# One-input reductions for the softmax shift, normalisation's short steps on GpSimd, and the attention output gathered with the heads inside

## The chip, the cores and the metric

One core of one Trainium2 chip runs the whole kernel. The metric is the device time of one launch in microseconds (us), lower is better. Work is spread over TensorE (PE), VectorE (DVE), ScalarE (ACT), GpSimd (POOL) and the DMA queue that SyncE (SP) fills; each has its own instruction stream and waits for the others by semaphores.

## The reference

A Macaron block on x of shape (4, 1024, 256) in float32: half a gated feed-forward network, attention, half the same network again.

```python
def ffn(x):                       # weights are ternary, 704 hidden units
    g = (x @ gate_w.T) * gate_s
    u = (x @ up_w.T) * up_s
    return (silu(g) * u) @ down_w.T * down_s
def attn(x):                      # 16 heads of 16, rotary embedding, causal
    q, k, v = heads(x @ Wq.T), heads(x @ Wk.T), heads(x @ Wv.T)
    q, k = rope(q), rope(k)
    att = softmax(q @ k.T / 4 + causal_mask)
    return (att @ v).merge_heads() @ Wo.T
x = x + 0.5 * ffn(layernorm(x))
x = x + attn(layernorm(x))
x = x + 0.5 * ffn(layernorm(x))
```

## The kernel before

**Pieces and their order.** The work is cut into pieces such as `pe_s` (scores), `act_exp` or `dma_oc`. `timetable()` gives each piece a place (a due time), a cost and the pieces it waits for; `Timetable.settle()` then plays the program through with these costs and writes for each of the five engines one fixed order. An engine runs its list strictly in order, so a piece whose input is late holds up everything behind it. Constants steer the result: `MODE_PLACE` (the price for TensorE of changing the array's shape), `WINDOW` (how far it may look ahead), `AHEAD` (how early the scores are due), and `WARM_SHARE`: where TensorE would be busy for less than that share, `warm()` puts in a filler, a product of the identity with itself (L848), whose result nobody reads.

**Stages.** Eight chunks of 512 rows go through the first FFN, with the projections of batch 0 laid into it. Then come 16 attention groups (4 batches, 4 groups of 4 heads), and eight chunks of the second FFN. Projections of the next batch are spread over the attention groups.

**Normalisation, `x_pass`.** Per chunk VectorE takes `bn_stats` (L1108) and `bn_aggr` (L1112) and adds EPS to the variance (L1115, piece `dve_va`); GpSimd raises it to -1/2 (L1246, `pool_rs`); VectorE multiplies mean and result (L1120, `dve_nb`); ScalarE normalises (L1015, `act_xn`) and TensorE transposes (L855). Each x is then split into a high part (ScalarE, XH) and a rest (VectorE, XL, L1125).

**One attention group.** TensorE computes the scores with rows as queries (L932, with mask products L942), only so that VectorE can take each row's maximum (L1200, `dve_max`). The negative maxima are split into a high part and a rest and transposed (`dve_nm`: L1209, L1212, L1214, L1219), written to memory (`dma_nw`, L1398) and read back as two extra rows of Q (`dma_nm`, L1405), against which K has two rows of ones. TensorE computes the scores again, transposed and already shifted (L957); ScalarE takes the exponential into PT (L1080); GpSimd zeroes the diagonal blocks (L1299, `pool_mask`); TensorE multiplies by V (L974), which also yields the row sums. There are eight PSUM banks for all of this.

**The way of the output.** ScalarE copies the result to OS (L1088). SP writes it to DRAM (`ow`, L1411), reads the row sums back (`rs`, L1418), VectorE takes their reciprocal (L1225, `dve_rc`), SP writes that (`rw`, L1424) and then issues `oc`: the outputs of four heads into OC and the reciprocals, repeated 16 times, into SC:

```python
src = OD[c2].rearrange("(h r) q -> h r q", h=4)
sy.dma_start(oc[r, :], src[:, 0:HD, :]).then_inc(sem, 16)
sy.dma_start(sc_[r, :], RD_[c2].unsqueeze(1).broadcast_to([4, HD, 512])).then_inc(sem, 16)
```

GpSimd multiplies the two (L1306, `pool_on`), ScalarE makes the high part (L1093, `act_lh`), GpSimd the rest (L1311), and TensorE projects. There are 16 such `pool_on` in the program. SP's queue also carries Q and K of coming groups (`ld`, L1391, 8 transfers of 192 KB a group) and the rotated projections (`zw`, L1380).

Of the kernel before, what the change touches and what calls it, by code (L numbers as in the profile page):

```python
# [9 lines left out]
F32R = mybir.dt.float32r  # L10
# [73 lines left out]
INNER = {"dve_va": ("dve_bn", "dve_ag"), "dve_nm": ("dve_mn", "dve_nh", "dve_nl"), "pool_r": ("pool_ts", "pool_tc"), "dve_flagint": ("dve_flagsum",)}  # L84
# [14 lines left out]
def s_width(t, ch):  # L99
    return 512 if ch < t // 4 else (t % 4 + 1) * P  # L100
# [31 lines left out]
class Timetable:  # L132
# [21 lines left out]
    def settle(self):  # L154
# [76 lines left out]
        while todo or ends:  # L231
# [12 lines left out]
            for e in self.order:  # L244
                while free[e] <= now:
# [53 lines left out]
MODE_PLACE, WAIT_NS, DMA_RATE, WINDOW = 1.14, 80, 200.0, 56.5  # L299
# [50 lines left out]
def timetable():  # L350
# [22 lines left out]
    def x_pass(who, c, at):  # L373
# [254 lines left out]
def macaron(nc, x_in, wgu, wd, wqkv, wo, gsc, usc, dsc, ident_in, cos_in, sin_in, mask_in, out):  # L628
    ctx = ExitStack()
    with ctx:  # L630
# [37 lines left out]
        NP = [place(f"NP{i}", [P, 2, BT, 4]) for i in range(2)]  # L668
        NM = [place(f"NM{i}", [P, 2, 2, 2, 2, 4], F32R) for i in range(2)]
# [154 lines left out]
        def shift_parts(gr, c2, part):  # L824
            return NM[gr % 2][:, c2, :, part, :, :].rearrange("p a b t -> p t a b")

# [165 lines left out]
        def scalar_program(e):  # L992
            sc = nc.scalar
            for piece in plan.order["ACT"]:
# [12 lines left out]
                elif kind == "act_xn":  # L1007
# [3 lines left out]
                    e.wait_ge("dve_nb", who, c)  # L1011
# [83 lines left out]
        def vector_program(e):  # L1095
            ve = nc.vector
            for piece in plan.order["DVE"]:
                kind, a = piece[0], piece[1:]
                if kind == "dve_va":
# [13 lines left out]
                    ins.then_inc(S["dve_ag"], 1)  # L1113
                    e.wait_ge("dve_ag", *a)
                    ve.tensor_scalar(VE[k], MV[k][:, :, 1], EPS, None, ALU.add).then_inc(S["dve_va"], 1)  # L1115
                elif kind == "dve_nb":
                    who, c = a
                    k = slot["ST", a]
                    e.wait_ge("pool_rs", *a)
                    ve.scalar_tensor_tensor(NB[k], MV[k][:, :, 0], -1.0, RS[k], ALU.mult, ALU.mult).then_inc(S["dve_nb"], 1)  # L1120
# [68 lines left out]
                elif kind == "dve_max":  # L1189
                    gr, t, ch, u, hh = a  # L1190
                    n, sel = s_width(t, ch), 0 if ch == t // 4 else 1
# [3 lines left out]
                    acc = NP[gr % 2][:, sel, t, :]  # L1195
                    if u == "a":
                        acc, src = acc[:, 2 * hh:2 * hh + 2], pair("pe_s", *a)[:, :, 0:n]
                    else:
                        acc, src = acc[:, 2 * hh + u:2 * hh + u + 1], bank("pe_s", *a)[:, 0:n]
                    ve.tensor_reduce(out=acc, in_=src, axis=AX, op=ALU.max, negate=True).then_inc(S["dve_max"], 1)  # L1200
                elif kind == "dve_nm":
                    gr, c2 = a
                    t = slice(4 * c2, 4 * c2 + 4)
                    np_ = NP[gr % 2]
# [3 lines left out]
                    if c2:  # L1208
                        ve.tensor_tensor(np_[:, 0, t, :], np_[:, 0, t, :], np_[:, 1, t, :], ALU.min).then_inc(S["dve_mn"], 1)  # L1209
                        e.wait_ge("dve_mn", *a)  # L1210
                    src = np_[:, 0, t, :].rearrange("p t (a b) -> p t a b", a=2)
                    ve.tensor_copy(shift_parts(gr, c2, 0), src).then_inc(S["dve_nh"], 1)  # L1212
                    e.wait_ge("dve_nh", *a)
                    ve.tensor_tensor(shift_parts(gr, c2, 1), src, f32(shift_parts(gr, c2, 0)), ALU.subtract).then_inc(S["dve_nl"], 1)  # L1214
# [328 lines left out]
```

## Time and profile before

| | |
|---|---|
| median of 3 runs | 898.68 us (896.30 to 898.89) |
| the profiled execution: time | 898.62 us |
| its span in the trace | 896.4 us |
| TensorE busy | 837.8 us, 93% of the span |
| VectorE busy | 642.5 us, 72% |
| ScalarE busy | 552.1 us, 62% |
| GpSimd busy | 376.6 us, 42% |
| DMA | 33.9% of 16 engines' span, 89.8 MB |

Busy time counts instructions that run, also while they are stretched by a wait inside them. Fillers count as TensorE busy. Times below are us from the start of the span, 2.2 us of the execution's time lie outside it.

### The profile page before, as it was taken

To read this page: it belongs to the slowest core of one execution; us is meant where nothing else is said; L and a number is where in the kernel's file an instruction comes from. 1 tells how busy PE (TensorE), PEld (TensorE's weight loads), DVE (VectorE), ACT (ScalarE), POOL (GpSimd) and SP (SyncE) were. 2 spreads that over 40 slices of the span, in tenths; PEclk is the share of its full clock that TensorE was granted. 3 is DMA by queue.
4 is the path that set the end of the run, shared out by engine and by line. 5 is a ranking of instruction groups with operands and counts; after the bars stand their busy time and mean duration, and the time that the engine had idled before them with its cause. 6 is when DMAs were issued, how large, how long until landed. Compare 5 with 4: busy or idle time off the path is not lost.

```text
span 896.4 us, 17613 instructions
## 1 busy us (share of the span) xinstructions
PE 837.8 (93%) x6446; PEld 572.6 (64%) x6446; DVE 642.5 (72%) x1305; ACT 552.1 (62%) x1064; POOL 376.6 (42%) x355
## 2 busy tenths in 40 slices
PE   5899999989998999999999999799999999999996
PEld 5788887775655565665555665345555556888885
DVE  5767678886987878888788778678888802565442
ACT  3755655446555747666767747467667886556642
POOL 1757675453332353351252541321332324555553
PEclk9999999999988979999899999799999999999999
DMA  9701232109345264461453615424641111001101
GB/s 313 288 1 68 74 106 85 25 3 225 115 140 153 58 167 125 150 153 64 101 151 126 180 38 157 110 65 87 206 103 50 45 44 37 24 24 36 36 24 49
DMA packets 64644, 89.80 MB, mean 100 GB/s; under 512 B 18604, under 2 KB 30252, under 8 KB 64300
## 3 DMA queue, kind: packets, MB, share of 16 engines
q1 hardware_dynamic: 64412, 88.57, 33.9%
q8 instruction: 54, 0.88, 0.4%
q14 instruction: 34, 0.28, 0.1%
q10 hardware_dynamic: 144, 0.07, 0.0%
HBM read 45.52 MB, written 40.76 MB: 96 GB/s over the span
## 4 chain that ended last, share of the span: by engine, by line
PE 59%; DVE 18%; ACT 8%; DMA 6%; issue 4%; SPq 2%; POOL 2%; DVEq 1%; POOLq 0%; ACTq 0%
PE psum L869 13%; PE psum L974 9%; DVE NP L1200 8%; PE psum L895 8%; PE psum L932 8%; PE psum L838 8%; PE psum L957 7%; DMA SC<-rd_ 3%; ACT PT L1080 3%; PE psum L848 2%; DVE ST L1108 2%; PE psum L855 2%; ACT XN L1015 2%; DVE HF_f L1151 2%; PE psum L942 2%
## 5 line engine op out<-in xcount | busy, mean ns | idle before, releaser
L1200 DVE TENSOR_REDUCE NP<-psum 128x1 f32<-128x512 f32 (+3 forms) x640 | 362.1, 627 | 70.5 <-PE psum L942 43.9
L1080 ACT ACTIVATE PT<-psum 128x512 f32<-128x512 f32 (+2 forms) x640 | 307.3, 577 | 151.5 <-PE psum L957 150.5
L1299 POOL TENSOR_SCALAR_AFFINE_SELECT PT<-PT 128x512 f32<-128x512 f32 x128 | 80.7, 638 | 235.0 <-ACT PT L1080 235.0
L932 PE MATMUL psum<-K,Q 48*128 48x512 f32 (+2 forms) x768 | 154.6, 419 | 9.6 <-DVE NP L1200 6.1
L957 PE MATMUL psum<-Q,K 50*128 50x512 f32 (+2 forms) x768 | 149.6, 417 | 13.8 <-ACT PT L1080 6.7
L869 PE MATMUL psum<-XH,WG_f 128*128 128x512 f32 x352 | 142.9, 406 | 9.6 <-DVE HF_f L1151 6.4
L974 PE MATMUL psum<-PT,V 128*32 128x512 f32 (+3 forms) x1536 | 150.1, 509 | 1.0 <-POOL PT L1299 0.9
L869 PE MATMUL psum<-XL,WG_f 128*128 128x512 f32 x352 | 138.4, 393 | 0.0
L1256 POOL TENSOR_TENSOR HL_f<-HF_f,HH_f 128x512 fp32r<-128x512 f32 x80 | 102.9, 1295 | 80.6 <-ACT HH_f L1044 80.4
L932 PEld LDWEIGHTS psum<-K,Q 48*128 48x128 f32 x768 | 75.2, 191 | 73.7 <-DVE NP L1200 36.9
L1151 DVE SCALAR_TENSOR_TENSOR HF_f<-psum,US,G_f 128x512 f32<-128x512 f32 x96 | 71.1, 750 | 61.2 <-ACT G_f L1034 35.4
L957 PEld LDWEIGHTS psum<-Q,K 50*128 50x128 f32 x768 | 73.9, 192 | 53.4 <-DVE NP L1200 16.8
L1044 ACT ACTIVATE HH_f<-HF_f 128x512 fp32r<-128x512 f32 x96 | 60.1, 630 | 52.4 <-DVE HF_f L1151 51.3
L895 PE MATMUL psum<-WD_f,HH_f 128*128 128x256 f32 x384 | 88.1, 284 | 3.8 <-DVE HH_f L1158 3.1
L1034 ACT ACTIVATE G_f<-psum,GS 128x512 f32<-128x512 f32 x96 | 65.0, 683 | 37.9 <-PE psum L869 37.2
L974 PEld LDWEIGHTS psum<-PT,V 128*32 128x32 f32 x1536 | 40.8, 111 | 71.7 <-issue 52.0
L848 PE MATMUL psum<-IDT 64*128 64x128 f32 (+1 forms) x428 | 77.4, 300 | 9.3 <-ACT PT L1080 5.7
L869 PEld LDWEIGHTS psum<-XH,WG_f 128*128 128x128 f32 x352 | 66.1, 188 | 29.8 <-DVE HF_f L1151 8.5
L895 PE MATMUL psum<-WD_f,HL_f 128*128 128x256 f32 x320 | 78.0, 280 | 0.0
L848 PEld LDWEIGHTS psum<-IDT 64*128 64x128 f32 (+1 forms) x428 | 65.9, 204 | 17.5 <-ACT PT L1080 9.2
L895 PEld LDWEIGHTS psum<-WD_f,HH_f 128*128 128x128 f32 x384 | 69.9, 189 | 7.6 <-issue 6.3
L869 PEld LDWEIGHTS psum<-XL,WG_f 128*128 128x128 f32 x352 | 66.2, 188 | 12.6
(75 smaller groups left out, 1072.6 us busy)
## 6 DMA issues: line engine op xcount, KB each, us to landing
zd<-ZH SPq DMA_DIRECT2D x32, 512.0 KB, 4.8
Q<-zd SPq DMA_DIRECT2D x64, 192.0 KB, 3.9
K<-zd SPq DMA_DIRECT2D x64, 192.0 KB, 5.0
zd<-ZL SPq DMA_DIRECT2D x16, 512.0 KB, 4.8
od<-OS SPq DMA_DIRECT2D x32, 256.0 KB, 3.5
OC<-od SPq DMA_DIRECT2D x32, 128.0 KB
SC<-rd_ SPq DMA_DIRECT2D x32, 128.0 KB
out<-X SPq DMA_DIRECT2D x16, 256.0 KB, 2.1
```

The lines of the kernel that those rows point to most:

```text
L838: ins = tn.matmul(dst, x, w, start=(m == 0), stop=(m == len(terms) - 1))
L848: tn.matmul(bank(*piece)[:, 0:P], IDT[r, :], IDT[r, :], start=True, stop=True)
L869: ins = tn.matmul(bank(*piece), f32(w) if general else w, f32(x) if general else x, start=(kt + m == 0), stop=(kt + m == 2))
L895: ins = tn.matmul(dst, f32(h) if general else h, f32(w) if general else w, start=(n == 0), stop=(n == len(terms) - 1))
L932: ins = tn.matmul(dst, Q[k][r, p, t * P:(t + 1) * P], K[k][r, p, ch * 512:ch * 512 + w], start=(m == 0), stop=not diag)
L957: ins = tn.matmul(dst, K[k][r, p, j * P:(j + 1) * P], Q[k][r, p, 512 * c2 + base:512 * c2 + 512], start=True, stop=True)
L974: ins = tn.matmul(bank(*piece)[32 * h:32 * h + 32, skip:512], V[b % 2][:, col:col + 32], pt_view(gr, c2, j)[:, h, :], start=(j == 0), stop ...
L1080: sc.activation(dst, src, ACT.Exp, scale=0.25).then_inc(S["act_exp"], 1)
L1151: ve.scalar_tensor_tensor(HF[ph][k][ul, :], bank("pe_u", *a)[ul, :], US[ul, i:i + 1], G[ph][k][ul, :], ALU.mult, ALU.mult).then_inc(S["dve ...
L1200: ve.tensor_reduce(out=acc, in_=src, axis=AX, op=ALU.max, negate=True).then_inc(S["dve_max"], 1)
L1256: gp_.tensor_tensor(HL[ph][s][:, :], HF[ph][slot[f"Gf{ph}", a]][:, :], f32(HH[ph][s][:, :]), ALU.subtract).then_inc(S["pool_hl"], 1)
L1299: gp_.affine_select(out=pt, in_=pt, compare_op=ALU.is_ge, fill=0.0, base=0, pattern=[[0, 4], [1, P]], channel_multiplier=-1).then_inc(S["p ...
```

## The change

Four edits. (1) Of `dve_nm` every step but the transpose becomes a `tensor_reduce` with one input: the minimum of two halves, the high part (which is now a negated copy, so one of K's two rows of ones becomes -1), and the rest as the sum over two neighbours. The maxima are written in the order in which they are transposed. (2) The addition of EPS and the product of mean and factor move from VectorE to GpSimd, into `pool_rs`, which now has four instructions; `dve_nb` is gone. (3) `rs`, `rw` and `oc` address their tensors with another outer index: position first, head second, and Wo's rows are permuted on the host to match. (4) In the planner the cost of some pieces and four constants change, and `SPARE` adds 3000 ns to the planned end of `dma_oc` and 1200 ns to that of `dma_rs`.

```diff
-INNER = {"dve_va": ("dve_bn", "dve_ag"), "dve_nm": ...
+INNER = {"pool_const": ("pool_ones",), "dve_va": ("dve_bn",), "pool_rs": ("pool_va", "pool_pw"), "dve_nm": ...
...
-                        end = dma_free + LAG[e]
+                        end = dma_free + LAG[e] + SPARE.get(piece[0][:6], 0)
...
-MODE_PLACE, WAIT_NS, DMA_RATE, WINDOW = 1.14, 80, 200.0, 56.5
+MODE_PLACE, WAIT_NS, DMA_RATE, WINDOW = 1.112, 80, 200.0, 52.283
+SPARE = {"dma_oc": 3000, "dma_rs": 1200}
-AHEAD = 4.3
-WARM_SPAN, WARM_SHARE, WARM_COLD = 2700.0, 0.59, 10000.0
+AHEAD = 4.439
+WARM_SPAN, WARM_SHARE, WARM_COLD = 2700.0, 0.567, 10000.0
...
-        add(at, 1900, "dve_va", who, c, ...
-        add(at, 1070, "pool_rs", who, c, after=[("dve_va", who, c)])
-        add(at, 110, "dve_nb", who, c, after=[("pool_rs", who, c)])
+        add(at, 1750, "dve_va", who, c, ...
+        add(at, 1400, "pool_rs", who, c, after=[("dve_va", who, c)])
...
                     if c2:
-                        ve.tensor_tensor(np_[:, 0, t, :], np_[:, 0, t, :], np_[:, 1, t, :], ALU.min)
+                        ve.tensor_reduce(out=f32(sh[:, 0, :]), in_=NP[gr % 2][:, :, :].rearrange("p s n -> p n s"), axis=AX, op=ALU.min)
...
-                    ve.tensor_copy(shift_parts(gr, c2, 0), src)
+                    ve.tensor_reduce(out=sh[:, 1, :], in_=f32(sh[:, 0, :]).unsqueeze(2), axis=AX, op=ALU.max, negate=True)
...
-                    ve.tensor_tensor(shift_parts(gr, c2, 1), src, f32(shift_parts(gr, c2, 0)), ALU.subtract)
+                    ve.tensor_reduce(out=f32(sh[:, 2, :]), in_=f32(sh[:, 0:2, :]).rearrange("p s n -> p n s"), axis=AX, op=ALU.add)
...
+                    gp_.tensor_scalar(VE[k], MV[k][:, :, 1], EPS, None, ALU.add).then_inc(S["pool_va"], 1)
+                    e.wait_ge("pool_va", *a)
+                    gp_.tensor_scalar(NB[k], MV[k][:, :, 0], -1.0, None, ALU.mult)
+                    gp_.tensor_tensor(RS[k], VE[k], NH, ALU.pow).then_inc(S["pool_pw"], 1)
+                    e.wait_ge("pool_pw", *a)
+                    gp_.tensor_tensor(NB[k], NB[k], RS[k], ALU.mult).then_inc(S["pool_rs"], 1)
...
-                    src = OD[c2].rearrange("(h r) q -> h r q", h=4)[:, HD, :].rearrange("h (a n) -> h a n", n=16)
+                    src = OD[c2].rearrange("(h r) q -> h r q", h=4)[:, HD, :].rearrange("h (a n) -> a h n", n=16)
...
-                    src = OD[c2].rearrange("(h r) q -> h r q", h=4)
+                    src = OD[c2].rearrange("(h r) q -> r h q", h=4)
...
-                    sy.dma_start(oc[r, :], src[:, 0:HD, :]).then_inc(sem, 16)
-                    sy.dma_start(sc_[r, :], RD_[c2].unsqueeze(1).broadcast_to([4, HD, 512])).then_inc(sem, 16)
+                    sy.dma_start(oc[r, :], src[0:HD, :, :]).then_inc(sem, 16)
+                    sy.dma_start(sc_[r, :], RD_[c2].unsqueeze(0).broadcast_to([HD, 4, 512])).then_inc(sem, 16)
```

All orders are settled anew. TensorE's list (of the branch that is taken) has 191 fillers where it had 214, and 1055 changes from one kind of product to the next where it had 1087.

Three places of the order. First VectorE at the start of the program; ROW holds the normalisation's small results, FL the flags that decide which of two branches TensorE takes. Before:

```order
1 L1108 BN_STATS ST_61<-X 128x6 x4
2 L1112 BN_AGGR MV_63<-ST_61 128x2 x4
3 L1115 TENSOR_SCALAR ROW<-MV_63 128x4
4 L1131 TENSOR_REDUCE FL<-RG 128x1 x4
5 L1120 SCALAR_TENSOR_TENSOR ROW<-MV_63,ROW 128x4
6 L1131 TENSOR_REDUCE FL<-RD 128x1 x2
7 L1135 TENSOR_SCALAR FL<-FL 128x6
8 L1108 BN_STATS ST_62<-X 128x6 x4
9 L1112 BN_AGGR MV_64<-ST_62 128x2 x4
10 L1115 TENSOR_SCALAR ROW<-MV_64 128x4
11 L1138 TENSOR_REDUCE CST<-psum 1x1
12 L1140 CAST FLAG<-CST 1x1
```

And of the change:

```order
1 L1111 BN_STATS ST_61<-X 128x6 x4
2 L1115 BN_AGGR MV_63<-ST_61 128x2 x4
3 L1127 TENSOR_REDUCE FL<-RG 128x1 x4
4 L1127 TENSOR_REDUCE FL<-RD 128x1 x2
5 L1121 TENSOR_TENSOR XL_82<-psum,XH_80 128x512
6 L1131 TENSOR_SCALAR FL<-FL 128x6
7 L1121 TENSOR_TENSOR XL_82<-psum,XH_80 128x512
8 L1134 TENSOR_REDUCE CST<-psum 1x1
9 L1136 CAST FLAG<-CST 1x1
```

The result that ScalarE waits for no longer stands on VectorE behind four flag reductions, and the second chunk's statistics stand behind the flag.

Second SP's queue at the ninth `pool_on` (batch 2, first pair of groups); OC and SC are the output transfers, Q and K the `ld` of a coming group. Before:

```order
145 L1424 DMA rd_<-RC_74 128x16
146 L1437 DMA OC_108<-od 64x1x512
147 L1438 DMA SC_109<-rd_ 64x1x512
148 L1437 DMA OC_102<-od 64x1x512
149 L1438 DMA SC_103<-rd_ 64x1x512
150 L1391 DMA Q_92<-zd 48x2x512 x2
151 L1391 DMA K_93<-zd 48x2x512 x2
152 L1391 DMA Q_92<-zd 48x2x512 x2
153 L1391 DMA K_93<-zd 48x2x512 x2
```

The change has the same eight rows at the same numbers, 146 to 153; only their addressing differs.

Third ScalarE at the same place; OH is `act_lh`, PT the exponentials. Before:

```order
353 L1080 ACTIVATE PT_97<-psum 128x512 x3
354 L1088 ACTIVATE OS_101<-psum 128x512
355 L1080 ACTIVATE PT_97<-psum 128x512
356 L1080 ACTIVATE PT_98<-psum 128x384 x2
357 L1093 ACTIVATE OH_111<-OC_102 128x512
358 L1080 ACTIVATE PT_98<-psum 128x384 x2
359 L1080 ACTIVATE PT_96<-psum 128x512 x2
```

And of the change:

```order
355 L1083 ACTIVATE PT_97<-psum 128x512 x3
356 L1091 ACTIVATE OS_101<-psum 128x512
357 L1083 ACTIVATE PT_97<-psum 128x512
358 L1083 ACTIVATE PT_98<-psum 128x384 x3
359 L1096 ACTIVATE OH_111<-OC_102 128x512
360 L1083 ACTIVATE PT_98<-psum 128x384
361 L1083 ACTIVATE PT_96<-psum 128x512 x2
```

OH moves back by one exponential.

## Rows read from the trace of the kernel before

**Rows 1.** The page: the chain that ended last, shares of the span by engine.

```profile
PE 59%; DVE 18%; ACT 8%; DMA 6%; issue 4%; SPq 2%; POOL 2%; DVEq 1%; POOLq 0%; ACTq 0%
```

**Rows 2.** Windows by stage: length, busy us (instructions) by engine, PEclk, DMA share, GB/s.

```profile
203.30:746.80 543.50, 514.79 (x4510) 298.08 (x4510) 422.59 (x864) 358.82 (x745) 177.99 (x198) 0.95 0.42 116
```

**Rows 3.** Timeline of TensorE: start, us, what [idle before <- releaser].

```profile
429.85 0.69 PE L957 MATMUL psum<-Q,K 50*128 50x384 f32 x2 [2.11 <-ACT OS L1088]
530.38 0.50 PE L957 MATMUL psum<-Q,K 50*128 50x256 f32 x4 [1.49 <-ACT PT L1080]
577.66 0.58 PE L848 MATMUL psum<-IDT 64*128 64x128 f32 x1 [5.73 <-ACT PT L1080]
```

**Rows 4.** Timeline, the stall at 572 us, SP, GpSimd and ScalarE.

```profile
565.16 0.51 SPq L1438 DMA_DIRECT2D SC<-rd_  x1
575.31 1.26 POOL L1306 TENSOR_TENSOR OC<-OC,SC 128x512 f32<-128x512 f32 x1 [8.88 <-DMA SC<-rd_]
576.60 0.63 ACT L1093 ACTIVATE OH<-OC 128x512 fp32r<-128x512 f32 x1 [5.70 <-POOL OC L1306]
```

**Rows 5.** Windows with only OC and SC under way, and with `ld`; columns as Rows 2.

```profile
596.50:600.00 3.50, 2.88 (x33) 1.85 (x30) 2.86 (x7) 1.30 (x4) 0.74 (x2) 1.00 0.27 90
603.00:608.00 5.00, 4.74 (x52) 2.89 (x48) 4.75 (x11) 4.08 (x10) 1.87 (x4) 1.00 1.07 203
```

**Rows 6.** Seven windows at TensorE's lower clock: four of them and the sum of all.

```profile
313.80:323.90 10.10, 10.05 (x57) 6.31 (x58) 6.85 (x15) 2.59 (x6) 6.17 (x6) 0.50 0.77 162
429.90:436.70 6.80, 6.80 (x40) 4.79 (x44) 3.61 (x6) 4.74 (x11) 2.82 (x5) 0.51 0.72 173
532.30:535.70 3.40, 3.40 (x20) 3.18 (x19) 0.42 (x1) 1.26 (x2) 2.82 (x4) 0.52 0.04 14
573.30:583.40 10.10, 5.74 (x30) 2.65 (x30) 2.74 (x5) 2.99 (x7) 4.89 (x6) 0.50 0.32 90
...
sum 47.40, PE 42.94 PEld 26.34 DVE 25.24 ACT 14.56 POOL 20.79; mean PE 6.13 PEld 3.76 DVE 3.61 ACT 2.08 POOL 2.97
```

**Rows 7.** Timeline of TensorE, the same product at either clock.

```profile
256.77 0.63 PE L838 MATMUL psum<-XL,WQH 128*128 128x512 f32 x1
...
303.73 0.40 PE L838 MATMUL psum<-XL,WQH 128*128 128x512 f32 x1
```

**Rows 8.** Timeline of TensorE, idle time that VectorE ended.

```profile
252.44 0.80 PE L932 MATMUL psum<-K,Q 48*128 48x256 f32 x4 [1.99 <-DVE NP L1200]
277.07 0.45 PE L932 MATMUL psum<-K,Q 48*128 48x384 f32 x2 [1.62 <-DVE NP L1200]
693.59 0.50 PE L932 MATMUL psum<-K,Q 48*128 48x512 f32 x2 [1.00 <-DVE XL L1125]
```

**Rows 9.** Lines of VectorE: ns min/median/max, first and last start.

```profile
L1214 DVE TENSOR_TENSOR NM<-NP,NM x32: 187/190/2251, 152.1 to 718.3; 128x16 fp32r<-128x16 f32 x32
L1225 DVE RECIPROCAL RC<-SU x32: 209/243/255, 231.8 to 755.4; 128x16 f32<-128x16 f32 x32
```

**Rows 10.** Timeline at the first stretched step.

```profile
249.16 2.36 POOL L1292 TENSOR_TENSOR ZL<-TR,ZH 128x1024 fp32r<-128x1024 f32 x1 [1.52 <-ACT ZH L1051]
249.32 2.25 DVE L1214 TENSOR_TENSOR NM<-NP,NM 128x16 fp32r<-128x16 f32 x1
```

**Rows 11.** Timeline at the start of the program.

```profile
0.80 0.10 POOL L1238 MEMSET CST<- 128x4 f32 x1 [0.29 <-POOLq L1537]
...
6.77 1.03 POOL L1246 TENSOR_TENSOR ROW<-ROW,CST 128x4 f32<-128x4 f32 x1 [3.94 <-DVE ROW L1115]
...
11.42 2.07 ACT L1015 ACTIVATE XN<-X,ROW 128x256 f32<-128x256 f32 x4 [8.89 <-DVE ROW L1120]
...
22.22 0.47 PE L869 MATMUL psum<-XH,WG_f 128*128 128x512 f32 x1 [1.22 <-ACT G_f L1034]
...
31.46 1.93 DVE L1115 TENSOR_SCALAR ROW<-MV 128x4 f32<-128x4 f32 x1
...
34.10 0.50 PE L869 MATMUL psum<-XH,WG_f 128*128 128x512 f32 x1 [2.20 <-DVE HF_f L1151]
```

More of the change, by code:

```diff
@@ L82 @@
            "dve_xo": "dve_out"}
-INNER = {"dve_va": ("dve_bn", "dve_ag"), "dve_nm": ("dve_mn", "dve_nh", "dve_nl"), "pool_r": ("pool_ts", "pool_tc"), "dve_flagint": ("dve_flagsum",)}
+INNER = {"pool_const": ("pool_ones",), "dve_va": ("dve_bn",), "pool_rs": ("pool_va", "pool_pw"), "dve_nm": ("dve_mn", "dve_nh", "dve_nl"), "pool_r": ("pool_ts", "pool_tc"), "dve_flagint": ("dve_flagsum",)}
 DMAS = {"dma_ld": 4, "dma_zw": 3, "dma_nm": 2, "dma_oc": 2, "dma_on": 2, "dma_sp": 2, "dma_w2": 2}
@@ L377, in x_pass @@
         st, xn, x = p.prior["ST", (who, c)], p.prior["XN", (who, c)], p.prior["XA" if (who, c // 2) == ("a", 0) else "X", (who, c)]
-        add(at, 1900, "dve_va", who, c, after=x_ready(who, c) + ([("act_xn",) + st] if st else []))
-        add(at, 1070, "pool_rs", who, c, after=[("dve_va", who, c)])
-        add(at, 110, "dve_nb", who, c, after=[("pool_rs", who, c)])
-        add(at + 2, 4 * 491, "act_xn", who, c, after=[("dve_nb", who, c)] + ([("pe_xT",) + xn + (1,)] if xn else []))
+        add(at, 1750, "dve_va", who, c, after=x_ready(who, c) + ([("act_xn",) + st] if st else []))
+        add(at, 1400, "pool_rs", who, c, after=[("dve_va", who, c)])
+        add(at + 2, 4 * 491, "act_xn", who, c, after=[("pool_rs", who, c)] + ([("pe_xT",) + xn + (1,)] if xn else []))
         for kt in range(2):
@@ L667, in macaron @@
         VE, RS, NB = ([ROW[:, i, n, :] for i in range(2)] for n in range(3))
-        NP = [place(f"NP{i}", [P, 2, BT, 4]) for i in range(2)]
-        NM = [place(f"NM{i}", [P, 2, 2, 2, 2, 4], F32R) for i in range(2)]
+        NP = [place(f"NP{i}", [P, 2, 16]) for i in range(2)]
+        SH = [place(f"SH{i}", [P, 2, 3, 16], F32R) for i in range(2)]
         NMT = [place(f"NMT{i}", [P, 32]) for i in range(2)]
@@ L822, in pt_view, with maxima_of @@
             return PT[(PT_USES * gr + s) % PTN][:, 4 * off:4 * off + 4 * w].rearrange("p (h n) -> p h n", h=4)
-        def shift_parts(gr, c2, part):
-            return NM[gr % 2][:, c2, :, part, :, :].rearrange("p a b t -> p t a b")
+        def maxima_of(gr, t, ch):
+            if t < 4:
+                return f32(SH[gr % 2][:, 0, 0, :]).rearrange("p (a b t) -> p a b t", a=2, b=2)[:, :, :, t]
+            return NP[gr % 2][:, ch, :].rearrange("p (a b t) -> p a b t", a=2, b=2)[:, :, :, t - 4]
         def tensor_program(e, todo, general):
@@ L1010, in scalar_program @@
                     was = prior["XN", (who, c)]
-                    e.wait_ge("dve_nb", who, c)
+                    e.wait_ge("pool_rs", who, c)
                     if was:
@@ L1112, in vector_program @@
                         ins = ve.bn_aggr(MV[k][:, i, :], ST[k][:, i, :])
[L1113 to L1120, printed above, removed]
+                    ins.then_inc(S["dve_va"], 1)
                 elif kind == "dve_xl":
@@ L1190, in vector_program @@
                     gr, t, ch, u, hh = a
-                    n, sel = s_width(t, ch), 0 if ch == t // 4 else 1
+                    n = s_width(t, ch)
                     e.wait_ge("pe_s", gr, t, ch, u)
@@ L1217, in vector_program @@
                         e.wait_ge(*turn_of("nw", gr - 1, c2))
-                    both = f32(NM[gr % 2][:, c2, :, :, :, :]).rearrange("p a b c t -> p (a b c t)")
-                    ve.transpose(NMT[c2][:, :], both).then_inc(S["dve_nm"], 1)
+                    ve.transpose(NMT[c2][:, :], f32(sh[:, 1:3, :]).rearrange("p s n -> p (s n)")).then_inc(S["dve_nm"], 1)
                 elif kind == "dve_rc":
@@ L1238, in gpsimd_program @@
                     gp_.memset(NH, -0.5)
-                    gp_.memset(f32(ONES[:, :]), 1.0)
+                    gp_.memset(f32(ONES[:, :]), 1.0).then_inc(S["pool_ones"], 1)
+                    e.wait_ge("pool_ones")
+                    gp_.memset(f32(ONES[0:1, :]), -1.0)
                     gp_.memset(ONE, 1.0).then_inc(S["pool_const"], 1)
```

23 lines of the change are left out of this document (10 added, 13 removed).

## The prediction

> **What bounds the kernel now.** I read the chain that ended last first [rows 1]: 59% of it is TensorE, 18% VectorE, 8% ScalarE, and 6% are transfers. TensorE is therefore the engine to watch, and the others matter where it waits for them. The windows by stage come next [rows 2]: in the 543.5 us of the attention groups TensorE counts as busy for 514.8, so 28.7 us are idle, and its mean clock there is 0.95 of full. These two things, idle time and the lower clock, are what an edit on other engines can give back; the products themselves stay the same. Then I looked in TensorE's own timeline for the idle stretches of a microsecond and more and for what stands behind each.
>
> Three of them have one story [rows 3]: 2.11, 1.49 and 5.73 us, 9.3 in all, each ended by ScalarE. The longest can be followed [rows 4]. SP issues the last SC transfer at 565.2. GpSimd stands still for 8.88 us and multiplies at 575.3; ScalarE, whose list has OH in front of further exponentials, has waited 5.70 us for it and runs OH at 576.6; only then do PSUM banks come free, and TensorE goes on at 577.7. So a small transfer of output that nobody needs soon holds the exponentials, because both engines run strictly in order. The other two stand behind ScalarE's copy or exponentials in the same way, before 429.85 and 530.38.
>
> Three others are ended by VectorE [rows 8]: 1.99, 1.62 and 1.00 us, 4.6 in all. Behind the first stands one step of `dve_nm` [rows 10]: L1214 handles 16 numbers per partition and takes 2.25 us, and it ends just as GpSimd's subtraction on 1024 columns (249.16 to 251.52) ends. Its usual time is 190 ns, its longest 2251 [rows 9], while the reciprocal with one input of the same size never takes over 255. So what stretches it is that it has two inputs in SBUF while GpSimd works, and maxima queue behind it.
>
> After such stalls TensorE runs slowly: seven windows, 47.4 us long together, show a granted clock of 0.50 to 0.52 [rows 6], the lower of the two levels (1.2 and not 2.4 GHz). One matmul takes 0.63 us there and 0.40 at the full clock [rows 7], so of busy time at the lower clock I count 1 - 0.40/0.63 = 0.37 as lost. Three windows follow the stalls behind ScalarE (6.80 + 3.40 + 5.74 = 15.9 us busy, 5.9 lost). The fourth, at 313.8 (10.05 us busy), follows a wait that no edit aims at. The rest, 42.94 - 10.05 - 15.94 = 17.0 us, follows the three stalls behind VectorE: 6.3 lost.
>
> **The change part by part.**
>
> *Gather with the heads inside (A).* While only OC and SC are under way, the DMA share is 0.27, which is four engines of 16 busy; with `ld` it is 1.07, all of them [rows 5]. The outer index of these transfers is the head, 4 of them. I take it that each head's 16 rows go to one engine, and that with 16 positions outside the same rows go to 16 engines: a quarter of the time. At 575 us four such transfers stood in the four queues, with `ld` behind them; SP's eight rows are the same after the change, so the load is the same and only its spread differs. In the 3.5 us of that first window at 0.27, four transfers of this kind are mostly done, so the two pairs need some 3.5 to 4 us on four engines and 1 on sixteen, where they now also share four engines with a full `ld`. The wait of 8.88 then shrinks to some 2 to 3 us, and `act_lh`, which ScalarE reaches 5.70 us before its input, no longer waits. `SPARE` adds little there: OH moves back by one exponential only. Elsewhere it plans `pool_on` later by its 3 us, which by itself would cover the two shorter stalls. Worth: 9.3 us of idle time + 5.9 of clock = 15.2. From below nothing (if it does not spread), from above this.
>
> The Trainium skill states such a rule in "DMA: Bandwidth & Descriptors", section "Why a DMA increments its semaphore by 16 and not by 1": the number of engines is the largest one up to 16 that divides the slowest dimension of both sides. By it the old form gets 4 and the new one 16, which would make term A whole; without it term A would be nothing. By the same rule the read of the shift (two parts outside) stays on 2 engines and its write on 4, so these keep their queueing. The 0.27 agrees for the old form; no run yet shows the new one.
>
> *One-input steps (B).* Per `dve_nm` three or four steps stay three or four steps. A one-input step of 16 numbers is not in the trace as a `tensor_reduce`; the nearest are the reciprocal at 243 ns and the two-input step's unhindered 190 [rows 9]. Over about 80 steps the bounds are nothing and 80 x 0.05 = 4 us on VectorE, which is 78% busy in the stage, so off the path by most: I take 0. What goes is the stretching: 4.6 us of idle time + 6.3 of clock = 10.9. From below nothing, if a one-input reduction waits as well.
>
> *Normalisation on GpSimd (C).* GpSimd runs three more short steps per chunk, 24 times. From below such a step costs what a 4-column memset costs, 0.10 us, from above what the power costs, 1.03 [rows 11]; both products are of the cheap kind, so I take 0.1 and with hand-overs 0.4 us a chunk. Behind it on GpSimd wait the pieces of the FFN and masks; it is 33% busy in the attention stage, so this is hidden, and where the cover is gone it would be 24 x 0.4 = 10 us, at the most. VectorE loses two steps and one hand-over. At the start this shows: ScalarE gets its first input at 11.42, after four flag reductions on VectorE; with GpSimd's product right after the power (6.77 + 1.03) it is there at about 8.3. TensorE's first real product does not come 3 us earlier, since the flag needs the last weights; of that I count 1.3. The 1.22 us before 22.22 go, because ScalarE's second normalisation now stands behind the first gate. Of the 2.20 before 34.10, 1.93 were one stretched addition of EPS on VectorE (31.46), which is gone: I count 2. Together 4.5; bounds 1 and 6.
>
> [...]
>
> *Planner (D).* 32 changes of product kind less and 23 fillers less. No row shows a change of kind alone: from below it costs nothing, from above as much as a whole product's 0.40 us [rows 7], together 12.8. Since the products stay, I take it near the lower end, and as 0. The fillers stood in time in which TensorE had nothing else; their loss costs nothing while the clock holds.
>
> *What is late next (E).* TensorE has other idle time in the stage: 28.7 less the 13.9 named is 14.8 us, in waits under 1.5 us for the same engines. A stall that is taken away lets TensorE run into the next of these earlier, and the whole order is drawn anew, so some stalls of the old kind will come at new places. Between nothing and all of A + B = 26.1, I take four tenths back, 10.4. This is the choice on which the size hangs most.
>
> Sum: -15.2 - 10.9 - 4.5 + 10.4 = -20.2 us. Against the profiled execution's own 898.6 (0.1 from the median of the runs) that gives 878.4; I forecast 878.
>
> **The rivals.**
>
> *The gather does not get faster (12%).* The 0.27 could be the pace of reading single rows from DRAM, or `ld` on the same queues could be what delays SC. For it: the wait of 8.88 us fell together with `ld`. Against it: the share is level at 0.27 with no `ld` under way. Then A is nothing: 898.6 - 0.6 x 10.9 - 4.5 = 888.
>
> *A one-input reduction is stretched as well (8%).* The change would not do what it says on VectorE. Against it stands the reciprocal's 255 at most. Then B is nothing: 898.6 - 0.6 x 15.2 - 4.5 = 885.
>
> *Nothing is given back (13%).* The stalls were independent. 898.6 - 30.6 = 868.
>
> *The clock falls more often: slower (8%).* With 23 fillers less a gap of 1 us may be followed by a low stretch where it was not before; now seven are. Place: the attention groups, before products that wait for maxima. At 0.37 us lost per busy microsecond at the lower clock, 54 us more of them, about what there is now once more, eat the whole gain, and 62 make it slower by 0.3%. If the mean clock in the stage fell from 0.95 to 0.85, the lower level would hold for 30% of 543.5 us and not 10%: 109 us more, 40 us lost, 898.6 - 20.2 + 40 = 918. Against it: six of the seven low stretches follow stalls of a microsecond and more that the edits remove.
>
> **How the numbers follow.** My forecast, 878 with its neighbours from 870 to 886, has 54%. The rivals above have 12, 8, 13 and 8%, and 5% are left for a gain that a new order eats to within 0.3%. That 0.3%, 2.7 us, is about what a measurement of this kernel can tell from no change; the runs before lie 2.6 us apart. Faster by more than it: 54 + 12 + 8 + 13 = 87%; same 5%; slower 8%. The range holds the forecast, the two partial cases and most of the case without giving back: 864 to 894.
>
> **What would show it.** DMA share near 1.0 and not 0.27 while only OC and SC run; GpSimd's wait for SC (8.88 at the longest) under 3 us, and no ScalarE wait for `pool_on` over 1 us. The three reductions of the shift at 150 to 250 ns with no instance over 300. First normalisation on ScalarE at 8 to 9 us, the first FFN product 1 us or more earlier, no idle stretch over 1 us at 30 to 36 us. A mean clock in the attention groups of 0.96 or more, that stage at about 527 us. The prediction is wrong if new stalls of 2 us and more stand in that stage, or if the clock is below 0.95 there.

## The result, and the profile after

| | before | after |
|---|---|---|
| median | 898.78 us (896.3 to 901.28, 4 runs) | 860.45 us (858.56 to 865.6, 4 runs) |
| the profiled execution: time | 898.62 us | 865.6 us |
| its span | 896.4 us | 863.6 us |

The ratio is 0.9567, 95% interval 0.9525 to 0.9608: 38 us less, where the prediction said 20 and its range ended at 864. The execution that was profiled is the longest of the four, with a mean clock of 0.987; two others had 0.995 and 0.996 and spans of 857.

The page of the changed kernel, busy time by engine and the chain that ended last [rows 1 before]:

```profile
PE 823.4 (95%) x6400; PEld 561.6 (65%) x6400; DVE 614.7 (71%) x1257; ACT 548.5 (64%) x1064; POOL 391.6 (45%) x428
PE 73%; DVE 13%; ACT 9%; issue 2%; POOL 2%; DMA 1%; SPq 1%; DVEq 0%; POOLq 0%; ACTq 0%
```

TensorE went from 59% to 73% of the chain, and transfers from 6% to 1%. The windows by stage say where it was gained (columns as Rows 2):

```profile
0.00:204.90 204.90, 186.74 (x1106) 156.46 (x1107) 135.95 (x292) 113.92 (x190) 129.55 (x142) 0.98 0.32 107
204.90:712.60 507.70, 494.75 (x4442) 282.64 (x4446) 410.20 (x852) 354.19 (x742) 179.29 (x213) 0.99 0.48 124
712.60:863.60 151.00, 141.88 (x857) 122.52 (x856) 68.60 (x113) 80.42 (x135) 82.78 (x74) 0.98 0.10 32
```

The attention groups take 507.7 us where they took 543.5 [rows 2]: 35.8 less, with 12.95 us idle where there were 28.7, and a clock of 0.99 where it was 0.95. The stages around them, 203.3 and 149.6 us before, are 1.6 and 1.4 us longer. The whole gain lies in the attention groups, and the normalisation's new place shows no gain in the two stages that do it most.

The way of the output, GpSimd, ScalarE and SP (timeline, the same ninth `pool_on` as in [rows 4]; SC's first transfer of the pair there is issued at 564.75):

```profile
564.75 0.59 SPq L1438 DMA_DIRECT2D SC<-rd_  x1
568.99 0.59 SPq L1438 DMA_DIRECT2D SC<-rd_  x1
573.04 1.27 POOL L1306 TENSOR_TENSOR OC<-OC,SC 128x512 f32<-128x512 f32 x1
574.35 0.63 ACT L1096 ACTIVATE OH<-OC 128x512 fp32r<-128x512 f32 x1 [1.49 <-POOL OC L1306]
```

GpSimd no longer waits for SC; its multiplication follows its masks at once. ScalarE still waits 1.49 us, for GpSimd's order and not for a transfer. Over the program, from the list of waits (us in total, times, longest):

```profile
POOL OC L1306 <- DMA SC<-rd_: 6.0, 3, 3.6
ACT OH L1096 <- POOL OC L1306: 5.8, 4, 2.6
```

Before, these were 38.1 us in 13 waits (the longest 11.0, and not the 8.88 that I took for it) and 17.4 us in 8. The longest of each is over the bound that the prediction gave (3.6 for 3 us, 2.6 for 1 us), though both sums fell to a third or less. The DMA share while OC and SC alone run (windows of one microsecond, columns as Rows 2):

```profile
538.50:539.50 1.00, 1.00 (x14) 0.72 (x16) 1.00 (x4) 1.00 (x3) 0.00 (x0) 1.00 0.58 164
566.00:567.00 1.00, 0.99 (x15) 0.63 (x16) 1.00 (x5) 1.00 (x3) 0.00 (x0) 1.00 0.63 150
566.00:566.25 0.25, 0.24 (x5) 0.17 (x2) 0.25 (x2) 0.25 (x2) 0.00 (x0) 1.00 0.97 156
```

Nine to ten of 16 engines are busy in the mean of such a microsecond and not four [rows 5]. The share near 1.0 that I had named holds for a quarter of a microsecond (the last row) and not for longer: SP needs 0.5 to 0.6 us to issue each of the two transfers. That the first is mostly done when the second starts is my reading, and no row separates the two.

The shift's steps (lines of VectorE, ns min/median/max, as Rows 9):

```profile
L1204 DVE TENSOR_REDUCE SH<-NP x16: 177/188/189, 187.1 to 681.7; 128x16 f32<-128x32 f32 x16
L1206 DVE TENSOR_REDUCE SH<-SH x32: 157/170/171, 149.5 to 681.9; 128x16 fp32r<-128x16 f32 x32
L1208 DVE TENSOR_REDUCE SH<-SH x32: 186/186/191, 149.7 to 682.1; 128x16 f32<-128x32 f32 x32
```

None of 80 lasts over 191 ns, where a two-input step lasted up to 2251 [rows 9]. The largest idle stretch of TensorE in the groups is 0.76 us, after the one of 3.11 with which they begin.

### The profile page after: what moved, and what is told of

It is laid out like the page before. It is cut to its first block, busy times and chain, and to the rows that moved or that the text cites. A ratio compares the mean times of both kernels' runs of the same rounds, so it can differ in the third digit from the quotient of the medians.

```text
span 863.6 us, 17536 instructions
## 1 busy us (share of the span) xinstructions
PE 823.4 (95%) x6400; PEld 561.6 (65%) x6400; DVE 614.7 (71%) x1257; ACT 548.5 (64%) x1064; POOL 391.6 (45%) x428
## 4 chain that ended last, share of the span: by engine, by line
PE 73%; DVE 13%; ACT 9%; issue 2%; POOL 2%; DMA 1%; SPq 1%; DVEq 0%; POOLq 0%; ACTq 0%
PE psum L872 15%; PE psum L977 13%; PE psum L935 10%; PE psum L841 10%; PE psum L898 9%; PE psum L960 9%; DVE NP L1196 4%; ACT PT L1083 3%; DVE SH L1196 3%; PE psum L851 3%; PE psum L945 2%; PE psum L858 2%; ACT XN L1018 2%; DVE ST L1111 1%; ACT G_f L1037 1%
## 5 line engine op out<-in xcount | busy, mean ns | idle before, releaser
L1196 DVE TENSOR_REDUCE NP<-psum 128x1 f32<-128x512 f32 (+2 forms) x448 | 260.3, 643 | 31.1 <-PE psum L945 22.0
L960 PE MATMUL psum<-Q,K 50*128 50x512 f32 (+2 forms) x768 | 147.2, 411 | 10.8 <-ACT PT L1083 7.9
L935 PE MATMUL psum<-K,Q 48*128 48x512 f32 (+2 forms) x768 | 146.8, 408 | 4.2 <-DVE SH L1196 1.3
L977 PE MATMUL psum<-PT,V 128*32 128x512 f32 (+3 forms) x1536 | 145.2, 496 | 0.2 <-ACT PT L1083 0.2
L1196 DVE TENSOR_REDUCE SH<-psum 128x2 f32<-128x256 f32 (+2 forms) x192 | 102.5, 590 | 16.2 <-PE psum L945 15.3
L935 PEld LDWEIGHTS psum<-K,Q 48*128 48x128 f32 x768 | 70.2, 184 | 66.3 <-DVE NP L1196 22.1
L960 PEld LDWEIGHTS psum<-Q,K 50*128 50x128 f32 x768 | 71.1, 187 | 53.9 <-DVE NP L1196 15.1
L851 PE MATMUL psum<-IDT 64*128 64x128 f32 (+1 forms) x382 | 67.9, 296 | 4.2 <-DMA IDT<-ident 3.4
```

The source lines that it names most:

```text
L851: tn.matmul(bank(*piece)[:, 0:P], IDT[r, :], IDT[r, :], start=True, stop=True)
L935: ins = tn.matmul(dst, Q[k][r, p, t * P:(t + 1) * P], K[k][r, p, ch * 512:ch * 512 + w], start=(m == 0), stop=not diag)
L960: ins = tn.matmul(dst, K[k][r, p, j * P:(j + 1) * P], Q[k][r, p, 512 * c2 + base:512 * c2 + 512], start=True, stop=True)
L977: ins = tn.matmul(bank(*piece)[32 * h:32 * h + 32, skip:512], V[b % 2][:, col:col + 32], pt_view(gr, c2, j)[:, h, :], start=(j == 0), stop ...
```

## The experiments

E1 to E4 ran on one chip in one series, likewise E5 to E8, E9 to E12, E13 to E16, and E17 and E18, each beside runs of the kernel before (898.1, 898.1, 899.4, 898.8 and 900.8 us). A ratio is to those runs, with its 95% interval in brackets. "Order of before" means that every piece stands where it stood and only operations or addresses differ.

**E1: the gather alone, order of before.**

```diff
-src = OD[c2].rearrange("(h r) q -> h r q", h=4)
+src = OD[c2].rearrange("(h r) q -> r h q", h=4)
```

(and the same for SC, `rs`, `rw`, and Wo's rows.) 

> The kernel before with the third edit alone (rs, rw and oc addressed with the position outside; Wo's rows permuted), every piece in its old place. Theory 1, the forecast's term A at full size: only the three stalls behind ScalarE go, 898.8 - 15.2 = 884, 4 us to either side. Theory 2, the slow spread also held the other transfers that share its engines (the shift's write and read, the loads): more than the named stalls goes, 875 or less. Theory 3, the gather matters little while the order is the old one, since the new order did the work: 892 or more. In all of them the DMA share with only OC and SC under way goes from 0.27 to about 1.

878.86 us, ratio 0.9823 (0.9765 to 0.9881): 10.7 to 21.1 us less, 16 in the middle and 19 by the medians. Term A's 15.2 stands within that, and so does a gain some us larger. TensorE's timeline shows what stayed:

```profile
253.01 0.50 PE L932 MATMUL psum<-K,Q 48*128 48x256 f32 x4 [1.99 <-DVE NP L1200]
276.27 0.44 PE L932 MATMUL psum<-K,Q 48*128 48x384 f32 x2 [1.60 <-DVE NP L1200]
353.43 0.51 PE L957 MATMUL psum<-Q,K 50*128 50x512 f32 x2 [1.49 <-DVE NP L1200]
```

The two long stalls behind VectorE are there almost to the hundredth (1.99 and 1.62 before, [rows 8]; its third, of 1.00, is 0.53), and the three behind ScalarE [rows 3] are gone. The third row shown here has its like in the trace of before and was not in my list. There it stands behind a stretched step too:

```profile
356.31 1.21 DVE L1214 TENSOR_TENSOR NM<-NP,NM 128x16 fp32r<-128x16 f32 x1
358.39 0.50 PE L957 MATMUL psum<-Q,K 50*128 50x512 f32 x2 [1.50 <-DVE NP L1200]
```

**E2: one-input steps alone, order of before.** The edit is the `dve_nm` part of the diff. 

> The kernel before with the first edit alone (the shift by one-input reductions), every piece in its old place. Theory 1, term B at full size: 898.8 - 10.9 = 888, 4 us to either side. Theory 2 (the gather does most): 893 or more, because steps stretched by GpSimd cost TensorE only the three stalls named, and their successors are late for other reasons. Theory 3, the new order did the work: 893 or more as well. In all of them no step of the shift lasts over 300 ns.

886.79 us, ratio 0.9876 (0.9828 to 0.9924): 6.8 to 15.4 less, 11 in the middle, term B's 10.9. The 80 reductions of the shift last 192 ns at the most. In the timeline the stalls behind VectorE are gone, that of 1.50 us too, and those behind ScalarE are left:

```profile
414.41 0.69 PE L960 MATMUL psum<-Q,K 50*128 50x384 f32 x2 [2.41 <-ACT OS L1091]
515.77 0.50 PE L960 MATMUL psum<-Q,K 50*128 50x256 f32 x4 [1.44 <-ACT PT L1083]
562.01 0.58 PE L851 MATMUL psum<-IDT 64*128 64x128 f32 x1 [4.64 <-ACT PT L1083]
```

This shows that the three reductions aren't stretched. It doesn't show that the number of inputs is what counts, since the edit replaced a copy (L1212) as well, which has one input. The trace of before has that copy held too, and so has the addition of EPS, with one input and a constant (lines of VectorE, as Rows 9, and the timeline of one case):

```profile
L1212 DVE CAST NM<-NP x32: 171/182/1303, 151.3 to 718.1; 128x16 fp32r<-128x16 f32 x32
L1115 DVE TENSOR_SCALAR ROW<-MV x24: 170/170/1930, 6.5 to 812.5; 128x4 f32<-128x4 f32 x24
393.63 1.29 POOL L1286 TENSOR_TENSOR TR<-TR 128x512 f32<-128x512 f32 x1
393.65 1.30 DVE L1212 CAST NM<-NP 128x16 fp32r<-128x16 f32 x1
```

**E3: both, order of before.** 

> The kernel before with the first and the third edit, every piece in its old place. If the two add up, it is before less the sum of the two single gains. With the forecast's give-back of four tenths it would be 883; with nothing given back 872.6 for the forecast's sizes. If it is below 866, the two edits explain nearly the whole result of 860 to 862 and the planner's part is small; if it is above 880, the new order gave more than either.

863.91 us, ratio 0.9641 (0.9590 to 0.9692): 27.7 to 36.8 less, 32 in the middle and 34 by the medians. The single gains add up to 27 by the ratios and 30 by the medians. So nothing is given back: with four tenths back even the upper ends of both single intervals, 36.5, would leave 22. Whether the two together are worth more than apart is within the spread. After the stretch of 2.62 us with which the groups begin there is none of a microsecond in them, and the profiled clock is 0.993.

**E4: SPARE and the constants alone.**

```diff
+                        end = dma_free + LAG[e] + SPARE.get(piece[0][:6], 0)
-MODE_PLACE, WAIT_NS, DMA_RATE, WINDOW = 1.14, 80, 200.0, 56.5
+MODE_PLACE, WAIT_NS, DMA_RATE, WINDOW = 1.112, 80, 200.0, 52.283
-AHEAD = 4.3
+AHEAD = 4.439
...
```

> The kernel before with SPARE and the new constants alone: no operation and no transfer changes, only the order. Theory 1 (forecast's term D is 0): 899, 4 us to either side. Theory 3 (the new order did much of the work): 885 or less. Between these, the order is worth something by itself, by planning pool_on 3 us later and so taking ScalarE's waits for it away.

881.88 us, ratio 0.9841 (0.9796 to 0.9887): 10.1 to 18.3 less, 14 by the ratio and 16 by the medians, with no operation changed but for 22 fillers less. ScalarE waits for `pool_on` 4.9 us in all where it waited 17.4, though OC and SC are addressed as before. The planner cures the same waits as the gather.

**E5: the changed kernel without the gather.** 

> The changed kernel without its third edit (rs, rw and oc with the head outside again), SPARE and constants kept. Alone in the old order the gather was worth 16 to 19 us, and the planner's edit alone 16. Theory 1, both remove the same waits (of ScalarE for pool_on): the gather is worth little in the new order, 861 to 868. Theory 2, the gather works by itself in any order: 861 + 16 = 877.

866.68 us: by the medians the gather is worth 6 us there and 19 in E1. The intervals of E5 (0.9532 to 0.9697) and of the changed kernel (0.9525 to 0.9608) overlap, so the 6 is not clear of nothing. ScalarE's waits for `pool_on` add up to 6.7 us. Theory 1.

**E6: the changed kernel with two-input steps.** 

> The changed kernel without its first edit (two-input steps of the shift again). Theory 1, a stretched step hurts in any order: 861 + 11 to 18 = 872 to 879. Theory 2, the new order doesn't place these steps beside GpSimd's long products: 861 to 866. Steps of over 1 us should stand in the trace in the first case, hardly any in the second.

875.54 us, 15 more. The stretching comes back in other places, on VectorE and then on TensorE:

```profile
452.16 2.29 DVE L1207 TENSOR_TENSOR NM<-NP,NM 128x16 fp32r<-128x16 f32 x1
455.33 0.50 PE L932 MATMUL psum<-K,Q 48*128 48x256 f32 x4 [2.13 <-DVE NP L1193]
```

So this edit is worth as much in the new order as in the old, if not more: neither order avoids the stretching.

**E7: the changed kernel with the normalisation's steps on VectorE.** 

> The changed kernel without its second edit (EPS and the product of mean and factor on VectorE, as before). Forecast's term C: 861 + 4.5 = 865.5. Rival: the edit is worth nothing or costs, since the first and last stage took 1.6 and 1.4 us more with it and GpSimd's short steps take 0.20 to 0.27 us and not 0.10: 858 to 862.

868.25 us, 8 more. It also has another order, since the planner's costs go with it, so this isn't the edit's worth alone; E9 is the clean one.

**E8: the changed kernel without SPARE.** 

> The changed kernel without SPARE, new constants kept. Theory 1, with the gather spread over 16 engines the transfer lands in time and the spare is not needed: 861, 3 us to either side. Theory 2, the spare moves pool_on and act_lh to where nothing waits: 866 or more.

867.83 us, 7 more, again with another order.

**E9 and E16: all three edits' operations in the order of before.** In `dve_nb`'s place VectorE does nothing:

```diff
+                elif kind == "dve_nb":
+                    continue
```

> The first three edits' operations and addressing complete, but every piece in the place that the planner of before gives it (dve_nb's place on VectorE stays empty). The clean test of term C on top of the two others, which stood at 863.9 without it. Forecast: C is worth 4.5, so 859.4. Rival 1: nothing, 862 to 866, since GpSimd's short steps take 0.20 to 0.27 us and give back what VectorE's hand-over saved. Rival 2: it costs, 867 or more, because GpSimd's masks and rests of the FFN wait behind it.

861.85 us (860.97 to 862.58). E16 is the same kernel in the next series, though its label speaks of fillers: 

> The three edits in the order of before (861.85), built once more as it stands, to see how far one kernel moves between two series: 861.9, 2 us to either side. It is the reference for the half-filler runs.

861.67 us. The normalisation's worth is the difference to E3, which ran in another series: 2 us by the medians (863.9 to 861.9 and 861.7), 6 and 2 by the ratios (0.9641 to 0.9576 and 0.9619). The intervals of E3 and E9 overlap, so it is between nothing and some 10 us. And the operations alone, with no new order at all, make the whole gain to within 1 us.

**E10: the same operations, order drawn anew with the old constants.** 

> The first three edits with the new costs of the normalisation in the planner, so that all orders are settled anew, but without SPARE and with the old constants. Theory 1, a redrawn order is as good as another once no transfer and no short step is late: 861, 3 us to either side. Theory 2, the constants were needed: 866 or more.

876.68 us, 15 more than E9. Its idle stretches don't tell why: those of 0.25 us and more, from 15 us on, add up to 22.8 us, and to 21.0 both in the changed kernel and in E9. The clock tells a part: its four executions have a mean clock of 0.983 to 0.987, E9's 0.990 to 0.994. The mean difference of 0.006 is 10 us more at the half clock, and at 0.37 some 4 us, by estimate. The fillers tell more. TensorE's group of fillers in E10 (busy us, mean ns, idle before):

```profile
L850 PE MATMUL psum<-IDT 64*128 64x128 f32 (+1 forms) x472 | 83.6, 296 | 4.4 <-DMA IDT<-ident 3.6 <-ACT PT L1082 0.6
```

And in the changed kernel:

```profile
L851 PE MATMUL psum<-IDT 64*128 64x128 f32 (+1 forms) x382 | 67.9, 296 | 4.2 <-DMA IDT<-ident 3.4 <-ACT PT L1083 0.2 <-DVE SH L1196 0.2
```

In E10 there are 15.7 us more of work that nobody reads (and 9.2 more than in E9, which has 74.4): either fillers cost time, or they hide idle time.

**E11 and E12: the changed kernel, one constant moved.**

```diff
-MODE_PLACE, WAIT_NS, DMA_RATE, WINDOW = 1.112, 80, 200.0, 52.283
+MODE_PLACE, WAIT_NS, DMA_RATE, WINDOW = 1.112, 80, 200.0, 53.0
```

```diff
-AHEAD = 4.439
+AHEAD = 4.3
```

> The changed kernel with WINDOW 53.0 in place of 52.283, a change of 1.4% that redraws the orders from about the second batch on and does nothing else. If the worth of the constants is a matter of which order happens to be drawn, this moves the time by several us, as leaving SPARE out did (867.8); if orders near it are alike, 861, 2 us to either side.

861.62 us. 

> The changed kernel with AHEAD 4.3 in place of 4.439, the value of before. Same question as with WINDOW: 861, 2 us to either side if orders are alike; 864 or more if the drawn order matters by itself; below 859 would show that the constants chosen are not the best near here.

870.3 us. One draw is as good as the changed kernel's, the other is 10 us worse.

**E13 and E14: every second filler from the 17th on left out, all else in place.** E13 of the changed kernel, E14 of E10. This leaves out no work of the reference.

```diff
-            todo = plan.order["PE"]
+            todo = [x for x in plan.order["PE"] if not (x[0] == "pe_warm" and x[1] >= 16 and x[1] % 2)]
```

> The changed kernel with every second filler from the 17th on left out of TensorE's list (84 rows of the program's), all other pieces of all engines in place. Theory F, a filler takes time that a product would have had: each is 0.18 us by its mean busy time in the trace (67.9 us for 382 records), half of them some 30 us less at the most, so 850 or less. Theory I, the fillers lie in idle time: 861, or slower by up to 10 if the clock falls in the holes that they leave.

864.16 us, 4 more. 

> The three edits with the redrawn order and the old constants (876.7), with every second filler from the 17th on left out. Theory F: its extra 15 us are the 90 more filler records (83.6 us against 67.9), so it falls to 861 to 866. Theory O, the order of the products itself is worse: 873 or more.

882.3 us, 6 more. Theory F falls twice: fillers lie in time in which no product is ready, and taking them out turns it into idle time (from 21.0 to 28.5 us in E13, from 22.8 to 33.4 in E14, counted as above). The clock fell with it: 0.982 to 0.987 in E13, where three of the changed kernel's four executions have 0.994 to 0.996, and 0.973 to 0.981 in E14, where E10 has 0.983 to 0.987. By the same estimate this costs about 5 us in each. E10's order has the more time without a product, and its fillers keep it out of the idle column.

**E15: SPARE with the old constants.** 

> The three edits with SPARE but the old constants. If SPARE is what mends the redrawn order (876.7), 861 to 865; if the constants do it, 873 or more; in between, both are draws of an order.

876.95 us, as E10. SPARE alone doesn't mend the redrawn order; the constants alone do in part (E8, 867.8), and both together wholly (860.5).

**E17 and E18: the gather split, E9's kernel.** E17 re-addresses `oc` alone, E18 `rs` and `rw` alone.

> All three edits in the order of before, but rs and rw with the head outside as before; only oc (OC and SC) has the position outside. If the large transfers are the cause, as the prediction reads the stall, it stays at 861.9, 2 us to either side. If the small ones are (they are followed by waits of VectorE and of the next transfer), 870 or more.

862.5 us. 

> The reverse: rs and rw with the position outside, oc with the head outside as before. If the large transfers are the cause, about 861.9 + 23 = 885; if the small ones are, 865 or less.

889.9 us. The large transfers are the whole of it, as far as the spread lets one see (E9 861.85). In E18's list of waits (us in total, times, longest) the chain of the prediction is back:

```profile
POOL OC L1308 <- DMA SC<-rd_: 38.4, 15, 9.1
ACT OH L1096 <- POOL OC L1308: 19.5, 10, 5.1
```

In E17's it is gone:

```profile
POOL OC L1308 <- DMA SC<-rd_: 8.6, 3, 6.4
ACT OH L1096 <- POOL OC L1308: 5.4, 4, 2.1
```

## Why the prediction was wrong, step by step

**The step that failed is E, "What is late next".** It took four tenths of A + B, 10.4 us, as given back. E3 and E9 show nothing given back: the terms' sum without E is 30.6, their operations in the order of before gained 37. The rival "nothing is given back" (13%) had the right mechanism and gave 868. What I argued for E was that a stall taken away lets TensorE run into the next and that a redrawn order brings new ones. The first is refuted by E3. The second is real, but it belongs to term D: E10 pays 15 us for a redrawn order with the old constants, and the chosen constants pay nothing.

**A, the gather: right** in mechanism, place and size (E1: 10.7 to 21.1 for 15.2). E17 and E18 show the cause by itself: `oc`'s outer index, and neither the two small transfers nor `ld`. The Trainium skill's rule in "DMA: Bandwidth & Descriptors", section "Why a DMA increments its semaphore by 16 and not by 1", speaks of the largest number up to 16 that divides the slowest dimension of both sides; by that rule the gather goes from 4 engines to 16, and shares of 0.58 and 0.63, which four engines can't reach, agree. Alone in the new order the edit is worth about 6 (E5), since SPARE and the constants cover the same waits: the prediction saw that for "the two shorter stalls" and added the terms all the same, which did no harm as D was 0.

**B, the one-input steps: size and place right, the reason not** (E2: 6.8 to 15.4 for 10.9; E6: 15 in the new order). I said that a step is stretched because it has two inputs in SBUF. The trace of before denies it: the copy L1212, with one input, lasted over 500 ns in 4 of 32 instances, each time beside a GpSimd instruction, and the addition of EPS, which my own term C called stretched at 1.93 us, has one tensor as input as well. The copy was held just ahead of two of the stalls that I counted (0.56 us at 275.31, 1.04 at 691.09, before 277.07 and 693.59). What the runs support is narrower: reductions aren't held. In the changed kernel 29 of the 80 started while GpSimd was in an instruction of over 0.5 us, 16 of these in a two-input one with 190 ns or more still to go, and no step lasted over 191 ns. Which property of a reduction does it was not tested. By my reason the copy could have stayed as it was; that the edit replaced it too was luck for the forecast.

**What A + B missed.** They came to 26.1 and together measured 32 to 34 (E3). The two pages say where. Products and fillers are the same 6446 instructions in both, so what TensorE's busy time lost it lost by the clock:

```profile
PE 837.8 (93%) x6446; PEld 572.6 (64%) x6446; DVE 642.5 (72%) x1305; ACT 552.1 (62%) x1064; POOL 376.6 (42%) x355
PE 821.1 (95%) x6446; PEld 564.0 (65%) x6446; DVE 629.7 (73%) x1305; ACT 550.0 (64%) x1064; POOL 376.3 (44%) x356
```

Busy time fell by 16.7 us, where the terms had 5.9 + 6.3 = 12.2 for the clock. The rest of the span, 896.4 - 837.8 = 58.6 and 861.9 - 821.1 = 40.8, fell by 17.8, where they had 13.9. Two places make up most of the difference: the lower clock from 313.8 on, 10.05 us of TensorE's time [rows 6], which I had called untouched by any edit (at 0.37, 3.7 us), and the 1.50 us before 358.39, which belong to B. The first is gone in E1, E2 and E3 alike; why a single edit elsewhere takes it away is not shown. The stretches under 1 us hardly changed: from 15 us on, those from 0.25 to 1 us were 14.7 us before and are 13.7 in E3.

**C, the normalisation: mechanism half right, size not settled** (4.5 forecast; E9 and E16 against E3 give 2 to 6, and the spread allows anything from nothing to 10). ScalarE's first input came when forecast, but see the start of the program (timeline):

```profile
8.57 2.08 ACT L1018 ACTIVATE XN<-X,ROW 128x256 f32<-128x256 f32 x4 [6.04 <-POOL ROW L1246]
14.40 0.19 PE L879 MATMUL psum<-FL,CST 128*1 128x6 f32 x2 [1.95 <-DVE FL L1131]
16.64 0.77 PE L872 MATMUL psum<-XH,WG_f 128*128 128x512 f32 x1 [0.96 <-issue]
17.20 0.63 PE L872 MATMUL psum<-XL,WG_f 128*128 128x512 f32 x1
...
22.90 0.40 PE L872 MATMUL psum<-XL,WG_f 128*128 128x512 f32 x1
35.85 0.66 PE L858 MATMUL psum<-IDT,XN 128*128 128x128 f32 x4 [1.25 <-ACT XN L1018]
```

The first product of the FFN starts at 16.64 and not at 17.96, 1.3 us earlier as said, but behind 1.95 and 0.96 us of idle time, and the products up to 22.3 take 0.63 us each: 5.7 us at the lower clock, 0.37 of it lost, is 2.1 us and more than the lead. Before, these products ran at 0.40 from the start. The 2.20 us before 34.10 are gone, but 1.25 us stand before 35.85, where the transposition waits for ScalarE's normalisation; this sign of the prediction failed. A short step on GpSimd costs 0.20 to 0.27 us and not the memset's 0.10:

```profile
L1241 POOL TENSOR_SCALAR ROW<-MV 128x4 f32<-128x4 f32 x24 | 6.5, 270 | 69.4 <-DVE MV L1115 68.7
L1243 POOL TENSOR_SCALAR ROW<-MV 128x4 f32<-128x4 f32 x24 | 5.4, 227 | 2.0
L1246 POOL TENSOR_TENSOR ROW<-ROW 128x4 f32<-128x4 f32 x24 | 4.8, 201 | 1.9
```

Three of them are 0.70 us a chunk, more than twice the 0.3 that term C had without its hand-overs.

**D, the planner: 0 forecast, about 1 measured** (861.7 and 861.85 against 860.45, in other series, so not clear of 0). The 0 came out by luck, as a balance of two large parts that I didn't see: a redrawn order costs 15 us (E10), and SPARE and the constants together give it back (E8, E15: neither alone). That fillers take no time from products is right (E13, E14); but the clock did not hold without them, which term D had left as a condition. To the kernel before, SPARE and the constants alone would have been worth 14 to 16 (E4), by the waits that the gather removes as well.

**The rivals.** The gather without effect: refuted by E1, E17, E18. One-input reductions stretched too: refuted by E2, though other steps with one input are stretched. The clock falling more often: refuted, 0.99 in the groups.

What stays open is which property of an order makes it 10 or 15 us worse. E10's groups take 521.8 us from the first shifted score to the start of the last product with V, the changed kernel's 514.9; E12 moves one constant by 3% and is 10 us worse. Against E9 the two pages divide E10's 14.8 us of span (875.2 and 860.4): TensorE is busy for 12.2 us more (835.1 and 822.9), 9.2 of them in fillers and 3.0 in the same products, which goes with the lower clock, and it isn't busy for 2.6 more (40.1 and 37.5). These are the signs of an order in which products are ready late, not its cause.

## What to carry to other kernels

Here two stalls with different causes held one engine, the order of work stayed fixed, and their worths added up: count such stalls one by one, include the lower clock behind each, and give nothing back without a row that shows what comes next. A redrawn order is a term of its own; here it was worth 15 us by itself, so test an edit of operations with the old order kept. Read fillers as idle time: two kernels with nearly equal idle columns differed by 15 us, and the filler group's busy time and the clock said so. Before giving a reason for a slow instruction, look at the longest instance of every small step on that engine: one line of the trace would have told that the number of inputs isn't it.

## What the runs showed of the hardware

A small VectorE instruction that should take 0.2 us can be held for up to 2.3 us beside a long GpSimd one. In these traces this befell `tensor_tensor` (2251 ns), `tensor_scalar` (1930), the copy (1303) and `scalar_tensor_tensor` (1273), and not the reductions of the shift (192 in E2), the reciprocal (255) or the transposition (214).

A lower clock needs no stretch of a microsecond ahead of it. In E10 the only stretch of over 0.25 us between 240 and 262 us was one of 0.59, and three windows tell the rest (columns as Rows 2):

```profile
250.20:253.60 3.40, 2.74 (x27) 1.75 (x27) 3.40 (x7) 1.48 (x4) 1.03 (x2) 1.00 1.06 260
253.60:257.00 3.40, 3.40 (x24) 2.92 (x24) 3.40 (x7) 1.80 (x5) 3.40 (x5) 0.70 1.01 384
257.00:260.40 3.40, 3.40 (x18) 0.69 (x17) 2.16 (x6) 0.00 (x0) 0.32 (x1) 0.50 0.08 24
```

TensorE was busy for 2.74 of 3.40 us in the first, and then ran at 0.50 (1.2 and not 2.4 GHz) though it was always busy. The power on GpSimd takes 1.04 us for 4 numbers per partition, five times a product of the same size.
